# Latent attention of a decoder block: scores in fp32 on 32-row tiles of TensorE, heads in 32-partition slots, in units of a head group and half the queries

## The reference, cut to what matters

```python
q = (x @ Wq.T).reshape(b, t, 16, 16).transpose(0, 2, 1, 3)
latent = layernorm(x @ Wdkv.T, ln_g, ln_b)
k = (latent @ Wuk.T).reshape(b, t, 16, 16).transpose(0, 2, 1, 3)
v = (latent @ Wuv.T).reshape(b, t, 16, 16).transpose(0, 2, 1, 3)
q, k = apply_rope(q), apply_rope(k)
scores = jnp.einsum('bhqd,bhkd->bhqk', q, k) / np.sqrt(16)
scores = jnp.where(causal, scores, -jnp.inf)
attn = jax.nn.softmax(scores, axis=-1)
out = jnp.einsum('bhqk,bhkd->bhqd', attn, v)
```

## Time and profile before

| | us |
|---|---|
| median of 3 runs | 2898.22 (2896.65 to 2900.44) |
| the profiled execution, its own time | 2899.45 |
| its span, first to last instruction | 2897.6 |
| PE busy | 2651.6 (92%) |
| DVE busy | 1506.8 (52%) |
| ACT busy | 1233.8 (43%) |
| GpSimd busy | 337.4 (12%) |
| granted TensorE clock, mean | 0.967 |

### The profile page before, as it was taken

One profiled execution on the slowest core, in us unless ns is written; L12 is line 12 of the kernel. 1 busy time (PEld: TensorE's weight loads), 2 busy tenths in 40 slices (PEclk: granted clock), 3 DMA queues, 4 the chain that ended last, 5 costly groups with the idle time before them and its releaser, 6 DMA issues.

```text
span 2897.6 us, 43591 instructions
## 1 busy us (share of the span) xinstructions
PE 2651.6 (92%) x14862; PEld 1626.2 (56%) x14863; DVE 1506.8 (52%) x3738; ACT 1233.8 (43%) x2620; POOL 337.4 (12%) x561
## 2 busy tenths in 40 slices
PE   7999997999999997999999987989999988987998
PEld 4565654445656544445656544445556554446997
DVE  3434468754333568744333568743443568743443
ACT  3444225653443325654443325644442425641221
POOL 1000013012000013012000022012000022013111
PEclk9999999999999999999999999999999999998999
DMA  2000000001000000001000000001000000032111
GB/s 93 12 12 1 15 1 1 1 13 41 12 11 1 15 1 1 1 13 41 17 6 1 15 1 1 0 13 46 12 6 1 15 1 1 0 124 87 55 54 39
DMA packets 32394, 56.38 MB, mean 19 GB/s; under 512 B 7108, under 2 KB 23570, under 8 KB 31858
## 3 DMA queue, kind: packets, MB, share of 16 engines
q1 hardware_dynamic: 27490, 41.33, 4.5%
q0 software_dynamic: 4752, 13.02, 1.2%
HBM read 40.01 MB, written 14.32 MB: 19 GB/s over the span
## 4 chain that ended last, share of the span: by engine, by line
PE 77%; DVE 12%; ACT 5%; issue 3%; POOL 2%; DMA 0%; SPq 0%; DVEq 0%; ACTq 0%; POOLq 0%
PE ps L939 9%; PE ps L911 8%; PE ps L884 8%; PE ps L869 5%; PE ps L929 5%; PE ps L1168 4%; PE ps L1258 4%; PE ps L1153 4%; PE ps L1272 4%; PE ps L894 4%; DVE arena L1526 3%; PE ps L1128 3%; PE ps L1031 3%; PE ps L824 3%; PE ps L1049 2%
## 5 line engine op out<-in xcount | busy, mean ns | idle before, releaser
L1360 DVE TENSOR_REDUCE neg_max<-ps 128x1 f32<-128x128 f32 (+7 forms) x256 | 194.0, 758 | 567.6 <-PE ps L914 567.3
L1526 DVE TENSOR_REDUCE arena<-ps 128x1 f32<-128x512 f32 (+3 forms) x768 | 376.4, 549 | 109.3 <-PE ps L1131 51.9
L774 ACT ACTIVATE arena<-ps 128x512 f32<-128x512 f32 (+3 forms) x768 | 320.3, 513 | 157.4 <-PE ps L1156 152.5
L939 PE MATMUL ps<-arena 128*128 128x512 f32 (+3 forms) x768 | 318.0, 501 | 4.6 <-ACT arena L660 0.5
L660 ACT ACTIVATE arena<-ps 128x512 f32<-128x512 f32 (+3 forms) x384 | 188.2, 490 | 295.3 <-PE ps L929 293.2
L1128 PE MATMUL ps<-arena 128*128 (+4 forms) x768 | 249.2, 335 | 52.1 <-DVE arena L1526 50.2
L911 PE MATMUL ps<-arena 128*128 128x512 f32 (+3 forms) x768 | 290.7, 490 | 4.4 <-ACT arena L669 4.4
L1153 PE MATMUL ps<-arena 128*128 (+4 forms) x768 | 245.0, 329 | 11.9 <-ACT arena L759 2.8
L884 PE MATMUL ps<-turned_t,arena 128*128 128x512 f32 x512 | 228.8, 600 | 1.1 <-ACT turned_t L631 1.1
L911 PEld LDWEIGHTS ps<-arena 128*128 128x128 f32 x768 | 139.1, 190 | 135.3 <-issue 114.8
L929 PE MATMUL ps<-ident,arena 128*128 128x128 f32 x1152 | 193.0, 278 | 20.8 <-ACT arena L648 11.4
(11 more groups left out here) (231 smaller groups left out, 4246.8 us busy)
## 6 DMA issues: line engine op xcount, KB each, us to landing
arena<-in_w_qkv SPq DMA_DIRECT2D x32, 384.0 KB, 3.1
arena<-in_w SPq DMA_DIRECT2D x2, 4096.0 KB, 16.8
xin<-in_x SPq DMA_DIRECT2D x5, 1024.0 KB, 5.2
xres_ids<-sorted_res SPq DMA_DIRECT2D x35, 129.0 KB, 2.1
xin<-sorted_rows SPq DMA_DIRECT2D x35, 128.0 KB, 2.0
w_out<-in_w_out SPq DMA_DIRECT2D x1, 1024.0 KB
out<-xin,out_row POOLq DMA_INDIRECT x35, 2.7
sorted_res<-xin SPq DMA_DIRECT2D x4, 129.0 KB, 2.2
```

The costliest lines, as they stand in the source:

```text
L774: nc.scalar.activation(mprobs_t[kb % 2][:, j, lo:hi], ps[:, 3 + use % 3, 0:hi - lo], ACT.Exp).then_inc(mexp_done, 1)
L939: nc.tensor.matmul(ps[:, 6 + g, lo:BANK], v_rows[par][:, kb, :], probs_t[u % 4][:, lo:BANK], start=(kb == 0), stop=True, skip_group_check= ...
L1360: nc.vector.tensor_reduce(neg_max[:, par, t:t + 1], ps[:, buf:buf + 2, :].rearrange("p a n -> p (a n)")[:, 0:n], AX.X, ALU.max, negate=Tru ...
L1526: nc.vector.tensor_reduce(max_part[:, j, t, c:c + 1], ps[:, u % 3, 0:n], AX.X, ALU.max).then_inc(ms_taken, 1)
```

## The change

- The bf16 parts and stacks go. `q_heads_t` and `k_heads_t` hold fp32 heads, 32 partitions (a slot) for a head, four heads in the 128 partitions. The slots are rope's output (`q_slots`, `k_slots`, 32 columns a head, set by five GpSimd memsets before), transposed in fp32: 8 uses of 4 transposes for the queries, before the latent's transposes, and 8 for the keys; ACT copies all 16 of them. The `keep_warm` calls of this stage go.
- A score chunk is one fp32 matmul with 32 rows, which lies in one of four row tiles of the array. No matmul adds a mask. The row for the maximum is row 0 of the slot (-1 on the key side), and the unsplit maximum is added to it in place (`take_max`).
- For the maxima the diagonal chunks are masked and reduced by one DVE instruction, `tensor_tensor_reduce`, with a mask of 128x512 (`causal_wide`). For the keys GpSimd sets the masked part of the exponentials to zero (`affine_select`, 32 a batch, 4 heads x 128 queries each).
- The work is cut in 8 units (head group, half of the queries): 4 units with 16 chunks and 4 items, 4 with 32 chunks and 8 items. An item is one key tile of one unit: two pairs of score matmuls (banks 3 and 4, then 5 and 6), two exponentials of two banks each, four products two items later, into bank 7. The maxima of unit u+1 are spread over the items of unit u, those of the first unit and 6 chunks more run ahead. The chunks' heads are ordered so that a pair of an item (heads 0, 1) is followed by chunks of heads 2, 3, and the other way round. From the second unit on the chunks rotate over banks 0 to 2, the first unit's over banks 0 to 6.
- The norm's statistics for the next batch (`row_stats`) move between two units on DVE, its scales between two units on GpSimd. `v_group` goes; SyncE's last weights wait for `mout_taken` instead of `vg_ready`.

```diff
+BUFS = 4
+UNITS = [(0, 0), (1, 0), (0, 1), (1, 1), (2, 1), (3, 1), (2, 0), (3, 0)]
+LEAD, TURN_LEAD, TAKE_LEAD = 6, 3, 4
+        bank = m % 7 if m < FIRST_CHUNK[1] else m % 3
...
+def chunks_by(n, block):
+    u = unit_of(FIRST_ITEM, n)
+    if u + 1 == len(UNITS):
+        return CHUNKS
+    i, more = n - FIRST_ITEM[u], FIRST_CHUNK[u + 2] - FIRST_CHUNK[u + 1]
+    blocks = 2 * (FIRST_ITEM[u + 1] - FIRST_ITEM[u])
+    return min(FIRST_CHUNK[u + 1] + LEAD + more * (2 * i + block + 1) // blocks, CHUNKS)
...
 PE
+                def max_chunk(s):
+                    g, j, t, c = max_chunk_of(s)
+                    m = chunk_count(s, TURN_LEAD)
+                    n = min(BANK, (t + 1) * P - c * BANK)
...
+                    if MAX_NEEDS[m] is not None:
+                        pe.wait_ge(ms_taken, b * MAX_SLOTS + MAX_NEEDS[m])
...
+                    rows_j = slice(SLOT * j, SLOT * (j + 1))
+                    nc.tensor.matmul(ps[:, MAX_BANK[m], 0:n], q_heads_t[rows_j, g, t * P:(t + 1) * P],
+                                     k_heads_t[rows_j, g, c * BANK:c * BANK + n], start=True, stop=True).then_inc(ms_done, 1)
...
+                def item_scores(n, pair):
...
+                    if n >= 1:
+                        pe.wait_ge(mexp_done, b * (2 * ITEMS) + 2 * n - 1 + pair)
+                    for j in range(2 * pair, 2 * pair + 2):
+                        rows_j = slice(SLOT * j, SLOT * (j + 1))
+                        last = nc.tensor.matmul(ps[:, 3 + j, 0:hi - lo], k_heads_t[rows_j, g, kb * P:(kb + 1) * P],
+                                                q_heads_t[rows_j, g, lo:hi], start=True, stop=True)
+                for n in range(ITEMS):
+                    if n == FIRST_ITEM[-2]:
+                        turn_max(len(UNITS) - 1)
+                    item_scores(n, 0)
+                    chunks(issued, chunks_by(n, 0))
+                    if n >= 2:
+                        item_products(n - 2)
+                    item_scores(n, 1)
+                    chunks(chunks_by(n, 0), chunks_by(n, 1))
...
 DVE
+                    if c < t // 4:
+                        nc.vector.tensor_reduce(part, ps[:, MAX_BANK[m], 0:n], AX.X, ALU.max).then_inc(ms_taken, 1)
+                    else:
...
+                        nc.vector.tensor_tensor_reduce(max_junk[s % 2][:, 0:n], ps[:, MAX_BANK[m], 0:n], causal_wide[:, BANK - n:BANK], 1.0,
+                                                       part if c == 1 else MASKED, ALU.add, ALU.max,
...
+                def take_max(u):
...
+                    nc.vector.tensor_tensor(q_half, q_half, ps[:, MAX_BANK[m], :], ALU.add).then_inc(ms_taken, 1)
```

More of the change, by code:

```diff
@@ L172, in decoder_block @@
         inv_sum = sb("inv_sum", [P, 2, NT])
-        ARENA = 29800
+        ARENA = 29400
         arena = sb("arena", [P, ARENA])
@@ L580, in _ @@
+                for u in range(len(UNITS)):
+                    if u == 5:
+                        self_scales(step, b, NORM_NEXT)
+                    keep_causal(u)
                 for h in range(2):
@@ new lines, in turn_max @@
+                def turn_max(u):
+                    m = turn_count(u, TURN_LEAD)
+                    pe.wait_ge(ms_taken, b * MAX_SLOTS + max(MAX_NEEDS[m], chunk_count(FIRST_CHUNK[u + 1] - 1, TAKE_LEAD) + 1))
+                    for t in range(HALF):
+                        last = nc.tensor.transpose(ps[:, MAX_BANK[m], t * P:(t + 1) * P],
+                                                   max_stack[:, u % 2, t, :, :].rearrange("p j e -> p (j e)"), ident[:])
+                    last.then_inc(ms_done, 1)
@@ new lines, in chunks @@
+                def chunks(first, end):
+                    for s in range(first, end):
+                        for u in range(len(UNITS)):
+                            if s == turn_at(u, TURN_LEAD):
+                                turn_max(u)
+                        max_chunk(s)
+                def item_scores(n, pair):
+                    u, g, c, kb = item_of(n)
+                    lo = max(kb * P, c * BANK)
+                    hi = (c + 1) * BANK
+                    if kb == 0 and pair == 0:
+                        pe.wait_ge(ms_taken, b * MAX_SLOTS + turn_count(u, TAKE_LEAD) + 1)
+                    if n >= 1:
[4 more added lines that the diff above has]
+                                                q_heads_t[rows_j, g, lo:hi], start=True, stop=True)
+                    last.then_inc(mst_done, 1)
@@ new lines, in item_products @@
+                def item_products(n):
+                    u, g, c, kb = item_of(n)
+                    lo = max(kb - 4 * c, 0) * P
+                    if kb == 0 and n > 0:
+                        pe.wait_ge(mout_taken, b * (2 * NG) + u)
+                    if kb // 4 == c:
+                        pe.wait_ge(mdiag_done, b * (NG * NT) + HALF * u + kb % 4 + 1)
+                    pe.wait_ge(mexp_done, b * (2 * ITEMS) + 2 * n + 2)
+                    for j in range(GROUP):
+                        last = nc.tensor.matmul(ps[SLOT * j:SLOT * (j + 1), 7, lo:BANK], mv_rows[:, kb, GROUP * g + j, :],
+                                                mprobs_t[n % BUFS][:, j, lo:BANK],
+                                                start=(kb == 0), stop=True, skip_group_check=True)
+                    last.then_inc(mpv_done, 1)
@@ L1215, in _ @@
+                for n in range(ITEMS - 2, ITEMS):
+                    item_products(n)
                 turn_rows(b, TURN_NEXT, self_rows)
@@ L1573, in _ @@
+                take_max(len(UNITS) - 1)
+                for h in range(2):
+                    normed_rows(b, NORM_NEXT, h, xin, self_rows, scale, rows_ready)
                 back_rows(1, minv)
```

452 lines of the change are left out of this document (169 added, 283 removed).

## The result

The changed kernel takes 2983.27 us (median of 4 runs, 2969.43 to 2990.88) where the kernel before takes 2899.33 on the same chip (4 runs): a ratio of 1.0286, 95% interval 1.0245 to 1.0326. It is slower by 84 us, and 177 us above the forecast of 2806. Its profiled execution took 2979.47 us.

A forecast was written before the change was run, and what follows sets the result against it. PE, busy 92%, was taken as the bound. Units summing to 158 us from 457.5 end at 615.5 instead of 638.5: 23 us a batch, 92 in four; 2899.45 - 92 - 1.2 = 2806, range 2700 to 2970.

The forecast's parts named there:

- The round of four: Score and maximum matmuls: four row tiles run side by side, 0.86 us a round of 512 columns.
- partial overlap: Rival, row tiles: a round costs 1.10 to 1.12 us instead of 0.86, change comes out even, 2899 to 2906; chance 0.09.
- weight loads one after another: Rival, row tiles: loads not hidden beneath their own tile's stream, 0.46 us more a round, 2966; chance 0.11.
- serial tiles: Rival: row tiles run one after another, 286 us a batch with products instead of 158, about 3290; chance 0.03.
- The bank wait: 32-chunk units: block A's second chunk waits for its bank until 1.8 us after B began, making 3.8 us.
- The rival that the wait doesn't bite: 32-chunk units go at DVE's pace, 18.5 us instead of 27.3, total 2686; chance 0.13.
- beside that: Preparation: GpSimd's larger memsets, about 6 us, lie beside other work; the first item can start at 457.5.
- (1,0) in 21.5 us: Unit of four items beside 32 chunks: DVE's 17.3 us and four pauses of about 1 us, 21.5 us.
- The rival of a lower clock: Waits in each item bring the half clock: 6.3 us for 3.8, some 90 us a batch, about 3150; chance 0.04.
- (0,1): Unit of eight items beside 32 chunks, forecast at 27.3 us.
- (0,0): First unit: no products in two items, two waits for a bank, 11 us.
- (2,0), the turn and (3,0): Last stretch to the copy: 10 us, then 2 for `turn_max` and `take_max`, then 9.5; 21.5 in all.

The follow-up runs named there:

- short_lead: Changed kernel with DVE reducing only 64 columns of the chunks issued ahead of the items and beside unit (0,0): 2938.42 us, one run, where the kernel before takes 2899.16.

## Why the prediction was wrong

- *Sign and size.* Forecast 23 us a batch saved, measured 18 lost. The range, 2700 to 2970, missed by 13 us.
- *The round of four*: right. Side by side within 0.02 us, 0.43 a pass. The rivals of partial overlap, of weight loads one after another, and of serial tiles fell. One piece of the weight-load rival is real: behind a change of tiling or a wait the second pass follows after 0.54 us instead of 0.43 (558.93 to 559.47 above, then 559.91; again behind the wait at 560.90), so 0.1 us twice an item, 1.7 a 32-chunk unit.
- *The bank wait*: right, 1.97 us for 1.8; short reductions take 3.1 of the 29.9 away, and no more, probably because a bank is still held while its own matmul runs. An item of (1,1) takes 4.01 us for 3.8, which over 8 items is about the 1.7 above, out of the 2.6 that the unit was missed by. The rival that the wait doesn't bite fell, and its own price was wrong: even with short reductions the unit takes 26.8, not 18.5.
- *`tensor_tensor_reduce` at the reduction's price*: right where it starts from a constant, nearly where it starts from a value in memory. It is two instructions; masked chunks of 384 columns follow one another at 0.48 us in the first case and 0.54 in the second, where the plain ones took 0.485. Of little weight.
- *`affine_select`*: right, 0.636 us (below the 0.7 to 1.5 of the forecast); PE waited for it four times, 1.8 us in all.
- *Preparation*: the step "beside that" failed. The memsets don't lie beside DVE's `xp`, they shut it out for 4.9 us. That is 4 to 5 us a batch, the 4.2 of the first item.
- *(1,0) in 21.5 us*: the step that failed, half of the miss. It took PE's clock as full in a unit where PE is led by DVE for eight chunks an item: streaming, banks and DVE's 17.3 were all priced at 1.00. Measured were 41.7 us at a mean clock of 0.58, and with short reductions 24.5 at 1.00 and 42.0 at 0.50. The rival of a lower clock had the mechanism, but I put it into all items alike, at 3150 us and a chance of 0.04, on the mean of 0.95 of the passes before. The unit with the worst ratio of chunks to items should have been asked for by itself; the earlier trace rows had a sign of it, 442.5 to 498.5, where DVE led and the clock was 0.91.
- *(0,1)*: 5.2 over, 2.6 as (1,1), the rest its first 5.9 us at the half clock that (1,0) left (0.91 in the mean).
- *(0,0)*: the waits for banks were right, 11.2 us for 11 in short_lead at a clock of 1.00; the 3.2 over in the first batch, and 9.4 in the third, go with a clock of 0.87 and 0.50 and full reductions, the same omission as in (1,0).
- *(2,0), the turn and (3,0)*: 3.5 over; (2,0) takes 12.1 for 10 at full clock, and 11.3 with short reductions. What the rest is stays open.

Open is how the 20 us of (1,0) divide between banks and clock to better than a few us, and what exactly makes the clock fall and come back: the runs show where, not by what rule. Not tested is whether full-array matmuls at DVE's pace would keep it.

## What to carry to other kernels

When work is cut into units, look for the unit with the most of the secondary work beside the least of the main work, and price it alone, its clock too: here one unit of eight made half of the miss. Reordering the units alone brought +3% to +1.9%; with the later memsets and the moved statistics it became -0.4%. Where an engine of small tiles is led by another's pace, ask for its granted clock, not for its busy share. Before a GpSimd memset is called hidden, look at what DVE does between SBUF and SBUF in those microseconds.
